# A mixture-of-experts block: expert choice moved into the attention pipeline in batches, rows scattered to one fixed region per expert

## What is computed

```python
h = _L0_tok_ref(x, L0_tok_W)
h = h + _L0_attn_ref(_layernorm(h, axis=-1), W_attn, b_attn, W_o, b_o)
h = h + _L0_ffn_ref(_layernorm(h, axis=-1), router_w, w1, b1, w2, b2)

# inside _L0_ffn_ref
logits = flat @ router_w.T
probs = jax.nn.softmax(logits.astype(jnp.float32), axis=-1)
top_w, top_i = jax.lax.top_k(probs, K)                 # K = 2 of E = 8
top_w = (top_w / top_w.sum(-1, keepdims=True)).astype(x.dtype)
for e in range(E):
    w_e = jnp.sum(top_w * (top_i == e), axis=-1)[:, None]
    h = jax.nn.gelu(flat @ w1[e] + b1[e], approximate=False)
    out = out + w_e * (h @ w2[e] + b2[e])
```

## Time and profile before

| | |
|---|---|
| median of three runs | 428.76 us (424.58 to 429.30) |
| the profiled execution | 429.13 us, of which the span is 427.0 us |
| busy, share of the span | PE 83%, PEld 77%, DVE 60%, ACT 50%, POOL 40% |
| mean granted TensorE clock | 0.895 |
| DMA | 42.79 MB, mean 100 GB/s |

### The profile page before, as it was taken

How to read it: one execution, slowest core, us unless ns; L and a number is a source line. 1 busy time by engine, 2 the same in 40 slices (tenths; PEclk the granted TensorE clock), 3 DMA queues, 4 the chain that set the end, 5 groups by cost and what they waited for, 6 DMA issues and landing times.

```text
span 427.0 us, 14485 instructions
## 1 busy us (share of the span) xinstructions
PE 356.2 (83%) x5558; PEld 329.8 (77%) x5558; DVE 256.3 (60%) x662; ACT 212.6 (50%) x431; POOL 171.0 (40%) x214
## 2 busy tenths in 40 slices
PE   4979899989989989897522189999999999999910
PEld 4979889879979989786422179999999999999810
DVE  3787368855856877876459634555555555555426
ACT  5767576775765777663330034444444444444400
POOL 9136221253353362232630244555555555554210
PEclk9999999977977999997555569999999999999985
DMA  8982023442331233236016021323312232222058
GB/s 257 342 252 85 18 56 88 129 122 53 90 112 46 81 111 111 51 108 176 3 47 174 9 48 48 87 58 86 83 54 82 59 86 75 66 50 49 29 192 334
DMA packets 29671, 42.79 MB, mean 100 GB/s; under 512 B 12384, under 2 KB 19408, under 8 KB 29608
## 3 DMA queue, kind: packets, MB, share of 16 engines
q1 hardware_dynamic: 25480, 33.37, 25.9%
q0 software_dynamic: 4128, 8.50, 7.2%
HBM read 30.23 MB, written 9.67 MB: 93 GB/s over the span
## 4 chain that ended last, share of the span: by engine, by line
PE 37%; issue 7%; DVE 6%; POOL 4%; DMA 3%; ACT 1%; SPq 0%; POOLq 0%; DVEq 0%; ACTq 0%
PE PSA L1218 19%; PE PSA L1233 14%; DMA W2h<-yrows 2%; POOL XF L473 2%; PE PSA L1237 2%; PE PSA L1185 2%; DVE PTR L920 1%; POOL REG L480 1%; DVE H L987 1%; DMA REG<-xrows,KBR 1%; POOL REG L479 1%; DVE VB L918 1%; DMA yrows<-KBR 1%; DVE VB L914 1%; PE PSA L1117 0%
## 5 line engine op out<-in xcount | busy, mean ns | idle before, releaser
L1218 PE MATMUL PSA<-YT,W1h 128*128 128x128 f16 x774 | 79.8, 222 | 1.3 <-ACT PTR L665 0.7
L1218 PE MATMUL PSA<-YT,W1l 128*128 128x128 f16 (+1 forms) x516 | 76.9, 222 | 0.0
L1233 PE MATMUL PSA<-W2h,PTR 128*128 x516 | 70.9, 246 | 0.3 <-DVE PTR L679 0.3
L1218 PEld LDWEIGHTS PSA<-YT,W1h 128*128 x774 | 64.8, 99 | 5.4 <-DVE YT L949 1.7
L510 POOL DMA_INDIRECT yrows<-KBR x43 | 43.0, 999 | 64.1 <-DVE KBR L964 64.1
L665 ACT ACTIVATE PTR<-PSA 128x768 f32<-128x768 f32 x43 | 34.8, 810 | 64.8 <-PE PSA L1218 64.8
L1233 PE MATMUL PSA<-W2l,PTR 128*128 x258 | 63.5, 246 | 0.0
L505 POOL DMA_INDIRECT REG<-xrows,KBR x43 | 41.8, 972 | 43.3 <-DVE KBR L941 25.6
L670 ACT ACTIVATE PTR<-PTR 128x768 f16<-128x768 f32 x43 | 36.3, 844 | 44.3 <-PE PSA L1237 44.3
L679 DVE SCALAR_TENSOR_TENSOR PTR<-PTR 128x768 f16<-128x768 f32 x43 | 41.2, 958 | 27.0 <-ACT PTR L670 27.0
L1218 PEld LDWEIGHTS PSA<-YT,W1l 128*128 (+1 forms) x516 | 50.6, 98 | 0.0
(11 more groups left out here) (162 smaller groups left out, 781.6 us busy)
## 6 DMA issues: line engine op xcount, KB each, us to landing
WSTG<-w SPq DMA_DIRECT2D x16, 384.0 KB, 3.4
WSTG<-w SPq DMA_DIRECT2D x16, 336.0 KB, 3.4
REG<-xt SPq DMA_DIRECT2D x12, 324.0 KB, 5.4
W1l<-xt SPq DMA_DIRECT2D x10, 324.0 KB, 7.2
VB<-VP SPq DMA_DIRECT2D x99, 19.1 KB
H<-hrows SPq DMA_DIRECT2D x6, 288.0 KB, 2.8
xrows<-REG SPq DMA_DIRECT2D x1, 1600.5 KB
hrows<-H SPq DMA_DIRECT2D x1, 1296.0 KB
```

Of the source, the lines that this page charges most:

```text
L1218: ins = nc.tensor.matmul(bank(2 * u + f // (FC // 2), 128, FC // 2 * ST_)[:, w:w + ST_], weights[a, c], YT[0:rows, at:at + ST_], start=k = ...
L1233: nc.tensor.matmul(bank(4 + u, ST_, C), GP[a][:, at:at + ST_], weights[b], start=(f, a, b) == (0, 0, 0), stop=False)
```

## The change

1. **Choice and ranks by batches inside the pipeline.** The tiles are put in six batches of 4, 4, 4, 4, 4 and 2 tiles. DVE picks the first expert of a batch in one step (`choose_first`), the second in the next (`choose_second`), and in the one after that takes PE's ranks (`rank`, `choose_ranks`) and works out the gates and each token's two target rows (`choose_slots`). This happens for batches 0 to 3 in steps 9 to 12, 13 to 16, 17 to 20 and 21 to 23; batch 4 is chosen ahead of step 24, and batch 5 after it. The running counts are carried from batch to batch in `SUMS`.
2. **Scatter instead of table and gather.** `xrows` now has a fixed region of 2304 + 128 rows for each expert, and 7 x 128 spare rows. POOL scatters the 108 rows of each tile twice, once for each expert chosen (44 indirect transfers), batches 0 to 2 inside the pipeline. After the counts are known, POOL writes 128 filler rows behind the last real row of each expert (8 indirect transfers). The table, its 0/1 matrices and its matmuls go.
3. **Steps load contiguous rows.** SP reads the first row of a step from SBUF into a register and issues a plain transfer of 128 rows (`fetch_rows`), which takes the place of POOL's 43 gathers. A row is 196 numbers instead of 194: it also carries the first expert and its token, from which DVE works out the target row of each result, with two more instructions in `rows_out`.
4. **The last six second norms** (`norm2_row`, `norm2_low` of tiles 16 to 21) run on DVE instead of POOL.
5. The constants for the routing are loaded ahead of the pipeline instead of in its drain, with a transfer of filler rows to DRAM.

The core of the diff:

```diff
             for i in range(-6, NT + DRAIN):
                 if has(i + 5):
                     norm1_low(i + 5)
                 for t in norm2_at(i - 1):
-                    norm2_low(t)
+                    if t < LASTS:
+                        norm2_low(t)
                 if has(i + 6):
                     norm1_row(i + 6)
                 for t in norm2_at(i):
-                    norm2_row(t)
+                    if t < LASTS:
+                        norm2_row(t)
+                for t in SCATTER_AT.get(i, []):
+                    scatter(t)
...
+            def scatter(t):
+                gp.wait_ge(route, ROUTE * [n for n, (a, b) in enumerate(RBATCHES) if a <= t < b][0] + ROUTE)
+                wait_lo(gp, t)
+                rows = real_rows(t)
+                for k in range(TOPK):
+                    gp.indirect_dma_start(out=xrows, out_offset=bass.IndirectOffsetOnAxis(ap=SLOTU[0:rows, k * NT + t:k * NT + t + 1], axis=0),
+                                          in_=RB[0:rows, t * ROW:(t + 1) * ROW], in_offset=None).then_inc(scattered, 16)
...
+            for t in range(LASTS, NT):
+                scatter(t)
+            gp.wait_ge(count, 1)
+            gp.wait_ge(unfilled_in, 16)
+            for e in range(E):
+                gp.indirect_dma_start(out=xrows, out_offset=bass.IndirectOffsetOnAxis(ap=FILLTO[:, e:e + 1], axis=0),
+                                      in_=UNFILLED[:, e * ROW:(e + 1) * ROW], in_offset=None).then_inc(filled[e], 16)
...
+        ROUTE, CHOOSE, EXPONENT, RANKED = 25, 14, 8, 17
+        FIRST_AT = {9: 0, 13: 1, 17: 2, 21: 3}
+        SECOND_AT = {10: 0, 14: 1, 18: 2, 21: 3}
+        SLOTS_AT = {11: 0, 15: 1, 19: 2, 22: 3}
+        SCATTER_AT = {12: [0], 13: [1], 14: [2], 15: [3], 16: [4], 17: [5], 18: [6], 19: [7], 20: [8], 21: [9], 22: [10, 11],
+                      23: [12, 13, 14, 15]}
+        LASTS = NT - 6
...
                 if has(i - 1):
                     y_lo(i - 1)
                 if i == 0:
                     refine(1)
                 if group_end(i - 2):
                     refine(group(i - 2))
+                for t in norm2_at(i):
+                    if t >= LASTS:
+                        norm2_row(t)
+                for t in norm2_at(i):
+                    if t >= LASTS:
+                        norm2_low(t)
+                if i in SLOTS_AT:
+                    choose_slots(SLOTS_AT[i])
+                if i in FIRST_AT:
+                    choose_first(FIRST_AT[i])
+                if i in SECOND_AT:
+                    choose_second(SECOND_AT[i])
...
             for i in range(NT + DRAIN):
+                if i == FIRST_NORM:
+                    dve.wait_ge(later_in, 16 * len(LATER))
+                if i == NT + DRAIN - 1:
+                    choose_first(4)
+                    choose_second(4)
                 step(i)
...
+            choose_ranks(4)
+            choose_slots(4)
+            choose_first(5)
+            choose_second(5)
+            choose_ranks(5)
+            choose_slots(5)
...
+            def fetch_rows(s):
+                need(sp, xr_mm, s - XRS + 1)
+                need(sp, target_done, s - XRS + 1)
+                need(sp, gate_done, s - XRS + 1)
+                if s < E:
+                    sp.wait_ge(filled[s], 16)
```

443 lines of the change are left out of this document (244 added, 199 removed).

## The result

| | before | after |
|---|---|---|
| median of four runs each | 426.67 us | 444.45 us (442.25 to 447.73) |
| the profiled execution, its span | 429.13, 427.0 us | 447.73, 445.6 us |
| mean granted clock in it | 0.895 | 0.872 |

The changed kernel is slower: ratio 1.042, with an interval of 1.031 to 1.053. Of 445 us forecast, 444.45 came. Ratios compare the least disturbed executions of both kernels. Where a group of experiments had the kernel before beside it, its median is given with them.

What follows compares the result with a forecast made beforehand. PE, without slack in the pipeline, was taken as the bound. Pipeline 2.7 + 3.8 + 8.8 = 15.3, plus 1.0 for drain and routing, made 16.3 on 429.1: 445 us, range 428 to 453.

Steps and rivals of the forecast that it cites:

- What bounds: In the pipeline steps PE is busy throughout and has no slack; a step takes 6.3 us.
- Choice on DVE, 0.9 a batch: Pipeline, batches 0 to 2: choose_first hidden, choose_second 1.1 us unless at half clock, slots with rank 0.9 a batch, 2.7 for three.
- upper bound of 4.9 us: Choice on DVE in the pipeline: the most a batch could cost if nothing is covered, 24 instructions of 0.22 us.
- Scatters on POOL, 1.9 twice: Steps 13 and 17: scatters queued ahead of norm2_low make PE wait in steps 14 and 18, 1.9 us each, 3.8 together.
- Clock, 4.8 and 4.0: Extra half-clock stretches expected after steps 14 and 18, costing 4.8 and 4.0 us, together 8.8.
- more idle than stood ahead of the fall: Step 14: PE idle 3.1 us instead of 1.2, more than before the fall after step 10, so the clock falls.
- the sign at the end: If POOL's low parts come in time, 3.8 us and the clock's 8.8 fall away, most of the forecast's sum.
- Drain and routing, +1.0: Drain to first expert rows: the 27 us chain goes, but drain delay, batch 4, POOL's queue and transfers replace it: +1.0 us.
- One or no extra stretch: Rival on the pipeline's clock: one extra half-clock stretch gives 442.5 us (chance 0.20), none gives 438.8 us (0.13).
- Scatters slowed by DVE: Rival: each of the drain's 12 scatters takes 1.56 us instead of 0.99, 6.8 more, 452 us; chance 0.07.
- Faster: Rival: DVE's norms shorten the drain, the choice falls into DVE's waits, first rows 5.1 us earlier, 424.0 us; chance 0.13.
- Experts: Expert steps: two more DVE instructions (0.45 us) per step and SP's fetches are hidden, with 1 us of cover.

Runs made afterwards that it cites:

- second profile of the changed kernel: The changed kernel run again with nothing altered, as a control: 454.87, 457.33 and 464.03 us, one execution of 1506.38; ratio 1.085.
- the choice alone: The changed kernel with all 32 token scatters of the pipeline moved behind its last step, DVE still choosing by batches: 461.18 us in a single execution.
- eight pairs of dummies: From the kernel before with two unread dummy scatters on POOL in every step 12 to 21; these are the pairs outside steps 13 and 17: 457.39 us, single execution.
- the first experiment: The changed kernel with the two scatters taken out of POOL's queue in steps 13 and 17, later tiles moved back: 442.71 us, ratio 1.035.

## Why the prediction was right, point by point

*What bounds.* Right: at full clock and with no new work the four steps from 13 take 26.45 us in three profiles, and 26.52 in a fourth with the unread matmuls. What lengthened them was waiting of PE or its clock.

*Choice on DVE, 0.9 a batch.* The first batch cost 0.4 us in the changed kernel, where the clock is halved in these steps (31.66 against 31.25), and 1.6 at full clock (28.23 less 26.61 of the kernel with its norms on DVE), where the prediction's terms give 1.1 + 0.9 = 2.0. In the second profile of the changed kernel, also at full clock there, it is 2.6, with the scatters of step 12. `choose_first` is hidden as said: with the choice alone the maximum of step 14 comes 8.0 us behind that of step 13 instead of 6.3, and PE waits 0.17 longer for the exponential. `choose_second` is not, at full clock: PE waits 1.0 us in step 11 and 1.66 in step 19 for the exponential behind it. (The upper bound of 4.9 us for 24 instructions of 0.22 should read 5.3; nothing rests on it.) The maxima of steps 12, 16 and 20 do start without idle time; those of 11, 15 and 19 keep 0.35 us of it.

*Scatters on POOL, 1.9 twice.* The place and the queue were right, the size was not: PE waited 4.74 and 4.2 us for the low part, not 2.5 (2.80 and 4.2 in the second profile). The missing term is the collision of L510 (in step 18 of L521, 1.88 us instead of 0.3) with DVE's weight pieces, 1.6 us each time, which the earlier trace rows don't show because there the pieces began at 153.08, when the low part was done. Whether the pieces meet an instruction ahead of the low part or behind it hangs on some tenths of a microsecond: in step 14 of the second profile they came behind it, and the wait was near the forecast. In the sum it is the changed kernel less the one without these scatters: 3.1 and 2.6, together 5.7 instead of 3.8. What the pairs in other steps cost is not parted: eight pairs of dummies and what came with them made some 4 us, 3.0 of them in step 20.

*Clock, 4.8 and 4.0.* Two more stretches came, in steps 14 and 18, in both profiles of the changed kernel. A stretch of 10.2 us costs 4.65 (31.25 less 26.61, the same steps of two kernels), but these two were 13.7 us long. At the same price for each microsecond that is 6.2 each, an estimate, so 12.4 instead of 8.8; then some 6 of the 18.6 us are waiting and work. Choice and clock of steps 13 to 20 together are what the kernel without the scatters behind refine lost against the kernel before: 6.8 and 5.8, 12.6 instead of 10.6 (8.8 and two batches of 0.9). How much of it is clock can't be parted to the tenth.

The step that failed in the reasoning on the clock is "more idle than stood ahead of the fall", and with it the sign at the end: that the clock's 8.8 fall away if POOL's low parts come in time. In the first experiment they came in time, and 6.8 and 5.8 us of loss stayed. A wait of 1.2 to 1.4 us in step 10 was followed by a fall in some executions and not in others, of one kernel too (the two profiles with norms on DVE: 31.25 and 26.61 for steps 9 to 12). And without the stall the clock fell as well, in steps 14 and 19 of two profiles. In step 19 the choice had made a wait of 1.66 us just ahead of the fall, which is the mechanism of the prediction in another place; in step 14 PE's waits had grown by 0.17 us only. Without new work it fell in steps 13 to 20 in none of three profiles. That the choice makes a fall likelier is what this suggests; what decides it is not shown.

*Drain and routing, +1.0.* It was -0.6. The rows of the changed kernel, DVE and then POOL and PE:

```profile
224.47 0.35 DVE L817 SCALAR_TENSOR_TENSOR H<-PSA,H 108x192 f32<-108x192 f32 x1
...
240.40 0.17 DVE L821 COPY LG<-PSA 108x8 f32<-108x8 f32 x1 [0.74 <-PE PSA L1220]
...
243.00 0.17 DVE L922 CAST SLOTU<-SLOTF 108x8 uint32<-108x8 f32 x1
```

```profile
243.47 0.99 POOL L529 DMA_INDIRECT xrows<-REG,SLOTU  x1 [0.83 <-DVE SAME L853]
...
258.93 0.99 POOL L558 DMA_INDIRECT xrows<-WSTG,FILLTO  x1 [0.30 <-issue]
...
264.62 0.50 PE L1293 MATMUL PSA<-IDH,REG 128*128 128x128 f16 x3 [18.08 <-DMA REG<-xrows]
```

The last logits are 15.9 us behind the residual of tile 20 (said: 16.4, before: 14.5), but only 2.4 later than before when counted from the maximum of step 21, not 4.1: the residual itself came 1.0 late and not 2.3. From there each term holds: slots 2.6 (2.7), twelve scatters 15.5 (15.5), filler to transpose 5.7 (5.8).

*The rivals.* "One or no extra stretch": two came. "Scatters slowed by DVE": the median of 44 is 0.99 us, the slowest 2.3, which a row of the line gives:

```profile
L529 POOL DMA_INDIRECT xrows<-REG,SLOTU x44: 897/986/2321, 141.0 to 257.7; - x44
```

The slowest two, 2.3 us at 141.04 and 1.7 at 177.78, ran beside DVE's weight pieces, so scatters can be slowed too; none of the twelve in the drain was, and nothing waited for those two. The price is in the tensor instruction behind the scatters. "Faster": its gain of the norms, 2 us in two profiles, is spent.

*Experts.* The scatters of result rows stay 3.64 us apart, and the rest of the span is 0.5 us shorter: hidden, as said.

So the forecast was 16.3, the difference of the medians is 17.8, and that of the two profiled spans 18.6: 16.3, less 0.5 for the first batch, plus 1.9 for the stalls, 2.0 for choice and clock, 1.0 ahead of step 9, less 1.6 for the drain and 0.5 behind it. The total was closer than its terms, and that is luck: the misses of +4.9 and -2.6 partly cancel. On the median of four runs, 426.67, the sum would have given 443.0. And the same kernel took 454.87 to 464.03 us when it ran again, above the range: its way from the maximum of step 21 to the first expert rows was 9.2 us longer than before, not 1.0, with a hole that no term of the sum has.

## What to carry to other kernels

In a pipeline that is bound by one engine, look at each wait that this engine already has. Here a step with 1.2 us of it is where new work on POOL's queue became longer waiting, and where the clock was mostly lost for 10 to 14 us more. When two parts of a change can each bring the clock down, taking one away wins little: try each alone on the kernel before. 64 unread matmuls in the short waits won 3.6 us here, where the whole rearrangement lost 18. And an instruction that is moved on POOL by 2.6 us meets other work of DVE; ask which, since the two can stand in each other's way for the full length of the DVE instruction.

## What was not expected of the hardware

- POOL instructions of 0.55, 0.30 and 1.01 us took 2.13, 1.88 and 2.55 us when DVE's two weight pieces (1.6 us together, two SBUF inputs) began within their first 0.1 us. A scatter of 0.99 that began during them took 2.32.
- The half-clock stretches are not a fixed property of a kernel: fifteen executions of the kernel before (those beside the first eight experiments, and the profiled one) spent 82 to 108 us of their span at half clock and took 421.9 to 435.0 us. Those with 103 to 108 took 433.0 to 435.0, two of the changed kernel with 104 and 105 took 440.1 and 440.9: at equal time at half clock the change costs some 6.5 us, and the rest of its 18 would be clock. This is an estimate, since PE is busy 5.61 of 27.04 us in the routing, where half clock should cost little, and the executions need not have their half clock at the same places; but it fits the 6 us that the stretches leave.
- 64 short matmuls in waits of 1.3 us and less took the spread of the time from 12 us (twelve executions) to 2.5 (eight).
- In one profile of the changed kernel and in one of a variant, on two chips, PE, DVE and ACT stood still together for 5.0 and 8.2 us with nothing to wait for that the profile names.
